# Layernorm statistics and scaling in a four-block tower: from whole-unit VectorE instructions to ScalarE instructions of 128x64

## What is computed

```python
def _layernorm(x, axis=-1, eps=1e-05):
    m = jnp.mean(x, axis=axis, keepdims=True)
    v = jnp.var(x, axis=axis, keepdims=True)
    return (x - m) / jnp.sqrt(v + eps)
...
h = _L0_tok_ref(x, L0_tok_W)
h = h + _L0_attn_ref(_layernorm(h), ...)   # linear attention with a decay mask
h = h + _L0_ffn_ref(_layernorm(h), ...)    # 16 experts, top 2, then a layernorm with gain and bias
h = h + _L1_attn_ref(_layernorm(h), ...)   # 2 heads in blocks of 8 tokens, softmax
h = h + _L1_ffn_ref(_layernorm(h), ...)    # 32 experts, top 1
h = h + _L2_attn_ref(_layernorm(h), ...)   # linear attention, two more layernorms with gain and bias
h = h + _L2_ffn_ref(_layernorm(h), ...)    # 8 experts, top 2, gelu
h = h + _L3_attn_ref(_layernorm(h), ...)   # complex diagonal recurrence
h = h + _L3_ffn_ref(_layernorm(h), ...)    # gated binary weights: signs of sums, "votes"
```

## Time and profile before

| | us |
|---|---|
| median of 3 runs | 701.21 |
| lowest and highest | 699.85, 702.47 |
| the profiled execution, whole | 703.61 |
| its span, first to last instruction | 701.8 |
| mean granted PE clock | 0.886 of full speed |

### The profile page before, as it was taken

How to read it: one execution, slowest core, us unless ns; L and a number is a source line. 1 busy time by engine, 2 the same in 40 slices (tenths; PEclk the granted TensorE clock), 3 DMA queues, 4 the chain that set the end, 5 groups by cost and what they waited for, 6 DMA issues and landing times.

```text
span 701.8 us, 8330 instructions
## 1 busy us (share of the span) xinstructions
PE 582.4 (83%) x2951; PEld 319.9 (46%) x2974; DVE 491.8 (70%) x921; ACT 298.4 (43%) x525; POOL 185.6 (26%) x146
## 2 busy tenths in 40 slices
PE   0378669999999999899589677685897999999996
PEld 0166345444335445366454453345543644444442
DVE  0857779966678998967787988878888973333331
ACT  0222231100011122545356445342455379999985
POOL 6783001000031313420527235425216220000000
PEclk9965569999999999998699887765999999999999
DMA  8310234689564530000000013200420000000011
GB/s 212 105 20 1 60 126 134 211 224 337 189 186 154 160 125 32 1 1 2 0 1 0 1 31 124 75 15 6 162 78 1 1 0 1 1 0 1 0 31 30
DMA packets 30777, 49.85 MB, mean 71 GB/s; under 512 B 8400, under 2 KB 8656, under 8 KB 30736
## 3 DMA queue, kind: packets, MB, share of 16 engines
q1 hardware_dynamic: 29136, 46.82, 21.3%
q10 hardware_dynamic: 576, 1.45, 0.9%
q0 software_dynamic: 1024, 1.05, 0.7%
HBM read 47.86 MB, written 1.44 MB: 70 GB/s over the span
## 4 chain that ended last, share of the span: by engine, by line
PE 54%; DVE 26%; POOL 6%; issue 6%; DMA 4%; ACT 3%; SPq 1%; DVEq 0%; another core or an unknown queue 0%
PE ps L771 9%; PE ps L1032 9%; PE ps L1010 7%; PE ps L764 6%; POOL inv_std L474 4%; PE ps L765 4%; DVE hid L1286 2%; DVE total L1181 2%; PE ps L759 2%; POOL sq L441 2%; DVE xn L1196 2%; PE ps L1021 2%; DVE var L1190 2%; PE ps L886 2%; PE ps L823 2%
## 5 line engine op out<-in xcount | busy, mean ns | idle before, releaser
L711 ACT ACTIVATE hid<-ps 128x512 bf16<-128x512 f32 x256 | 134.0, 619 | 30.4 <-PE ps L1032 29.2
L474 POOL TENSOR_TENSOR inv_std<-var,neg_half 128x8 f32<-128x8 f32 x44 | 79.1, 1798 | 192.1 <-DVE var L1190 191.7
L1032 PE MATMUL ps<-xs,w3z 128*128 128x512 f32 x256 | 118.2, 535 | 5.5 <-DVE xs L1488 3.1
L764 PE MATMUL ps<-xs,up_hi 128*128 128x512 f32 x192 | 97.1, 506 | 21.2 <-DVE hid L1286 13.7
L1010 PE MATMUL ps<-hid,kbin 128*128 128x512 bf16 x248 | 96.2, 391 | 1.0 <-ACT hid L711 0.5
L1488 DVE TENSOR_TENSOR xs<-ps,big_a 128x512 fp32r<-128x512 f32 x64 | 43.5, 689 | 75.3 <-PE ps L1021 72.1
L765 PE MATMUL ps<-xs,up_lo 128*128 128x512 f32 x192 | 79.6, 415 | 0.0
L764 PEld LDWEIGHTS ps<-xs,up_hi 128*128 128x128 f32 x192 | 37.8, 197 | 91.3 <-issue 40.8
L771 PE MATMUL ps<-hid,kb 128*64 128x512 f32 x256 | 69.5, 633 | 0.0
L620 ACT ACTIVATE hid<-ps,kd 128x512 f32<-128x512 f32 x64 | 43.0, 685 | 59.3 <-PE ps L765 34.8
L1032 PEld LDWEIGHTS ps<-xs,w3z 128*128 128x128 f32 x256 | 49.8, 195 | 29.6 <-ACT hid L711 13.1
(11 more groups left out here) (252 smaller groups left out, 973.9 us busy)
## 6 DMA issues: line engine op xcount, KB each, us to landing
big_a<-gates_out SPq DMA_DIRECT2D x64, 256.0 KB, 3.9
fm<-gates_out SPq DMA_DIRECT2D x32, 256.0 KB, 3.9
xT<-gates_out SPq DMA_DIRECT2D x32, 256.0 KB, 3.9
big_a<-gates_out SPq DMA_DIRECT2D x32, 128.0 KB, 2.9
fm<-gates_out SPq DMA_DIRECT2D x16, 128.0 KB, 2.9
xT<-gates_out SPq DMA_DIRECT2D x16, 128.0 KB, 2.9
hid<-wup SPq DMA_DIRECT2D x4, 391.0 KB, 12.5
out<-h SPq DMA_DIRECT2D x4, 256.0 KB, 2.6
```

The lines of the kernel that those rows point to most:

```text
L474: G.tensor_tensor(inv_std[u][:, :], var[u][:, :], neg_half[:, :], ALU.pow).then_inc(norm_rstd[u], 1)
L711: act.activation(sg[u][:, n % SUMS, :], b0, ACT.Sign).then_inc(s_made[u], 1)
L764: pe.matmul(b0, up_hi[:, a:a + P], xs[u][:, l, :], start=True, stop=False)
L1032: pe.matmul(b0, w3z[:, j, 2 * b:2 * (b + 1), :].rearrange("p i o -> p (i o)"), xs[u][:, l, :], start=True, stop=True).then_inc(w_made[u], 1)
```

## The change

The variance and most of the scaling are done elsewhere, and the lists are new:

- `square` now issues eight ACT instructions of 128x64, one for each sequence, in place of one of 128x512 (44 times: four units, eleven layernorms). Each has a bias read from a 128x1 tile, `eps_root`, and an accumulator output: the sum over its 64 elements goes to one column of `var`. The bias is sqrt(1e-5 / 64), so that the squares come with the epsilon.
- DVE's sum of the squares (L1190) is gone, all 44. POOL's `rstd` waits for ACT's last square.
- `square_scale` is `square` and a second step with eight ACT copies of 128x64, in place in `xn`, each with its scale read from a 128x1 column of `inv_std`. It serves A0, M0, A1, M1, A2, IN2, M2, A3 and M3; DVE's L1196, 36 instructions, is gone. IN0 and OUT2 keep DVE's multiplication.
- `sq` loses its 65th column, and POOL's setup fills `eps_root` once where it filled that column in four tiles.
- All five strings of `TURNS` are new.

```diff
--- before.py
+++ after.py
+EPS_ROOT = (LN_EPS / 64.0) ** 0.5
...
     "ACT": (
-        "sss00100211100031222011011ttt323322333232300000100110110011021020110302003020123011301322101002112321311"
+        "sss0000020202002200ttt1123121312233321121133331310300000000000000000202002022020012020133121312130322031"
...
+        eps_root = sb("eps_root", [P, 1])
...
-        sq = per_unit("sq", [P, SEQS, D + 1])
+        sq = per_unit("sq", [P, SEQS, D])
...
-        NORM_SUM, NORM_CEN, NORM_VAR, NORM_OUT, NORM_N = 1, 2, 3, 4, 4
+        NORM_SUM, NORM_CEN, NORM_OUT, NORM_N = 1, 2, 3, 3
...
-                    for n in units:
-                        G.memset(sq[n][:, :, D:D + 1], LN_EPS)
+                    G.memset(eps_root[:, :], EPS_ROOT)
                     G.memset(neg_half[:, :], -0.5).then_inc(eps_set, 1)
...
                     def rstd(ln):
                         yield
-                        pool.wait_ge(norm_step[u], norm_at(ln, NORM_VAR))
+                        pool.wait_ge(norm_sq[u], ln + 1)
                         G.tensor_tensor(inv_std[u][:, :], var[u][:, :], neg_half[:, :], ALU.pow).then_inc(norm_rstd[u], 1)
...
                     def square(ln):
                         yield
+                        if ln == LN_A0:
+                            act.wait_ge(eps_set, 1)
                         act.wait_ge(norm_step[u], norm_at(ln, NORM_CEN))
-                        act.activation(sq[u][:, :, 0:D], xn[u][:, :, :], ACT.Square, scale=float(D) ** -0.5).then_inc(norm_sq[u], 1)
+                        for j in range(SEQS):
+                            last = act.activation(sq[u][:, j, :], xn[u][:, j, :], ACT.Square, scale=float(D) ** -0.5,
+                                                  bias=eps_root[:, :], accum_out=var[u][:, j:j + 1])
+                        last.then_inc(norm_sq[u], 1)
+
+                    def square_scale(ln):
+                        yield from square(ln)
+                        yield
+                        act.wait_ge(norm_rstd[u], ln + 1)
+                        for j in range(SEQS):
+                            last = act.activation(xn[u][:, j, :], xn[u][:, j, :], ACT.Copy, scale=inv_std[u][:, j:j + 1])
+                        last.then_inc(norm_step[u], 1)
...
-                    yield from square(LN_A0)
+                    yield from square_scale(LN_A0)
...
                         V.scalar_tensor_tensor(xn[u][:, :, :], spread(total[u][:, :], D), -1.0 / D, src[u][:, :, :],
                                                ALU.mult, ALU.add).then_inc(norm_step[u], 1)
-                        yield
-                        if u == 0 and ln == LN_A0:
-                            dve.wait_ge(eps_set, 1)
-                        dve.wait_ge(norm_sq[u], ln + 1)
-                        V.tensor_reduce(var[u][:, :], sq[u][:, :, :], X, ALU.add).then_inc(norm_step[u], 1)
 
                     def norm(ln, src, ready, value):
                         yield from centred(ln, src, ready, value)
-                        yield
-                        dve.wait_ge(norm_rstd[u], ln + 1)
-                        V.tensor_tensor(xn[u][:, :, :], xn[u][:, :, :], spread(inv_std[u][:, :], D),
-                                        ALU.mult).then_inc(norm_step[u], 1)
```

More of the change, by code:

```diff
@@ L59 @@
+        "30320320121021031023023123102103102302312310210310230213210320103102321302102301021320320120310320123123"
+        "23131212312323131212312323131212312323131212312323131212312323131212312323131212312323123113133131131331"
+        "3113131333"
     ),
     "PE": (
[L61 to L62 removed]
@@ new lines @@
+        "20302310231313001301301311310331213123312313130213013320330011213132030231022322212221123220213320012311"
+        "13102312302131321302131300130133020302300201101303131320302011012033302020021200221001320020020230030022"
+        "00100210231003100110032001301100330012003130012301300200130032000310030000100210320000100320010320022002"
+        "23002200302200200221002200220120023200122001300221102231100223110023311002233100223310122331100223110023"
+        "31100223130022331012233110022311002331100221330022110332211003322003112003311002213302211330022110022330"
@@ L81 @@
+        "30031333333000020223000000000000000222020222222010110033302220222121010013311313101130323030330000002121"
+        "22201022202222222313321222122133030302212121111111120131131112333323131313131313230333333323221110131323"
+        "21312322021232232111203223331110111133221113023333313131032330121130332103210321032102301230123123123123"
+        "123123123123131313"
     ),
@@ L225, in view @@
             return ap[:, a:a + n].rearrange("p (j e) -> p j e", **sizes)
-        y = [sq[u][:, :, 0:D] for u in units]
+        y = [sq[u][:, :, :] for u in units]
         shifted = [view(fm2[u], 0, W, e=D) for u in units]
@@ L629, in program @@
                     act.activation(v[u][:, :, 0:LANES * D], per_tile(b0), ACT.Copy).then_inc(act_step[u], 1)
-                    yield from square(LN_M0)
+                    yield from square_scale(LN_M0)
                     yield from turned_parts(X_M0)
@@ L639, in program @@
                     yield from square(LN_IN0)
-                    yield from square(LN_A1)
+                    yield from square_scale(LN_A1)
                     yield from turned(X_A1)
@@ L655, in program @@
                     act.activation(wbd[u][32:64, :, 32:64], s32[u][32:64, :, :], ACT.Copy).then_inc(act_step[u], 1)
-                    yield from square(LN_M1)
+                    yield from square_scale(LN_M1)
                     yield from turned_parts(X_M1)
@@ L667, in program @@
                     act.activation(fm[u][:, :], b1, ACT.Relu).then_inc(act_step[u], 1)
-                    yield from square(LN_A2)
+                    yield from square_scale(LN_A2)
                     yield from turned(X_A2)
@@ L678, in program @@
                     act.activation(kf2[u], per_tile(b0), ACT.Relu).then_inc(act_step[u], 1)
-                    yield from square(LN_IN2)
+                    yield from square_scale(LN_IN2)
                     yield
@@ L686, in program @@
                     yield from square(LN_OUT2)
-                    yield from square(LN_M2)
+                    yield from square_scale(LN_M2)
                     yield from turned_parts(X_M2)
@@ L697, in program @@
                     act.activation(fm[u][:, :], b1, ACT.Copy).then_inc(act_step[u], 1)
-                    yield from square(LN_A3)
+                    yield from square_scale(LN_A3)
                     yield from turned_parts(X_A3)
-                    yield from square(LN_M3)
+                    yield from square_scale(LN_M3)
                     yield from turned(X_M3)
```

41 lines of the change are left out of this document (15 added, 26 removed).

## The result

| us | before | after |
|---|---|---|
| median of 4 runs, same chip | 700.53 | 725.73 |
| lowest and highest | 697.67, 702.47 | 722.70, 728.25 |
| the profiled execution's span | 701.8 | 726.0 |

The account below looks back on a forecast made before the run. No single engine was taken to bound the kernel: PE bounds the second stretch, ACT takes DVE's lead in the third. +3 - 9 + 2 - 5 = -9 us gave 694.6 us on the profiled execution, 692 by the median, range 666 to 718.

Parts of the forecast that it names:

- A square: On ACT, one 128x64 square with accumulator output was to hold the engine 0.35 us, eight 2.8 us.
- A product: On ACT, one 128x64 product with its scale read from a tile was to take 0.25 us, eight 2.0 us.
- 2.9 us more: Each layernorm's added latency from ACT's squares and products, said to hide while other units have work on every engine.
- 0 to M0: First stretch, to unit 3's layernorm M0: one layernorm's latency shows at A0, where nothing runs beside it, +3 us.
- M0 to A1: Second stretch, experts of the first block: PE bounds and loses 8.6 us of work to the new lists, -9 us.
- A1 to M3: Third stretch, 272 us before: ACT replaces DVE as fullest engine, so DVE's relief buys nothing; 274 us, +2.
- leaders' sum: Third stretch cut in six parts: busy times of each part's fullest engine added, 234 us forecast against 232.3 before.
- The share of it: Third stretch: the fullest engines' summed busy time over its length, 0.854 before, assumed the same after the change.
- M3 to the end: Last stretch, only votes: 215 instead of 223 stand behind unit 3's M3, at 0.60 us each, -5 us.
- the rival: The slower case: ACT's square groups stand before other units' activations or signs, so PE waits; 714 us, chance 0.27.
- ACT's bursts set the pace: Third stretch: square groups on ACT delay other units' activations and signs, +21 to +33 us; 714 us, chance 0.27.
- ACT stays cover: Third stretch: short instructions fit ACT's gaps and PE sets the time, -20 in place of +2; 670 us, chance 0.22.
- no effect: Third stretch held by unit order and latencies, ACT's longer chain cancelling DVE's relief; 701 us, chance 0.09.

Follow-up runs that it names:

- experiment 6: Kernel before with five memsets of 128x512 on POOL ahead of each power, nothing added on ACT, DVE or PE: 803.19 us, ratio 1.1489.
- the power in parts: Kernel after with POOL's power cut in two or four, each part started when its squares are done: 710.66 us (two), 713.76 us (four).

## Why the prediction was wrong

**The durations were right.** A square 0.35 forecast, 0.33 measured (bounds 2.0 and 3.7 us for eight, measured 2.65). Its accumulator step 0.10, measured 0.09. A product 0.25 and 0.24. ACT's busy time 475 and 461 us, DVE's 434 and 436. The four new table loads take 1.28 us each.

**The step that failed** is "2.9 us more, with POOL's 1.8 us unchanged between the earlier trace rows. While the other units have work on every engine this hides." The 2.9 us were about right (2.7 in the median, 2.1 in the mean), but they don't hide: experiment 6 has 104 of 126 us of such latency in the time with the lists of before, and the power in parts gives back 0.3 to 0.6 us for one with the lists of after. The forecast also left out that ACT now stands in front of its products while POOL works, 20 us in all. The premise was wrong, because cover needs an engine that may take up other work while one unit is late. Here the next instruction of PE's list is fixed, and if it is a transpose that waits for a product, all that stands behind it waits too. The kernel before said so: its rows for L759 had 26 us of PE waiting for products in a chain of 6.7 us, and the forecast didn't ask what this row does when the chain grows.

**0 to M0:** +3 forecast, +10.5 measured. Only A0 of one unit was charged, though this stretch holds seven whole layernorms and the start of the eighth, and PE is busy there for only 68 of the 115 us. With the lists of before the stretch is 120 us, five longer, and with those of after 123.5 even with the old code, so most of this goes with the lists.

**M0 to A1:** -9 forecast, -5.4 measured. Sign and cause right: PE binds there, and it has 9.1 us less to do (171.0 to 161.8); its idle time there rose from 10.0 to 13.8 us.

**A1 to M3:** +2 forecast, +14.6 measured. The leaders' sum was forecast at 234 us and is 238.0 (35.79 + 58.96 + 31.48 + 27.31 + 57.38 + 27.12). The share of it fell from 0.854 to 0.830: the sum's 4 us are worth 5, and the lower share 8. A share carried over from the kernel before assumes that the waits between engines stay as they are, and it was the waits that the change altered. PE leads four of the six parts, where the recorded sum took 33, 54, 33, 28 and 57 us of ACT and 29 of DVE and none of PE, although PE led two of them before; that 234 is near 238 is luck in part. PE's 227.6 us are 11 more than before, at a granted clock of 0.79 and not 0.84 (11 missing rows of before are up to 4 of them). The old code with the new lists has 226.9 us at 0.80 there, so this goes with the lists. Its stretch is 281 us long: of the 14.6 us some 9 come with the lists and 5.5 with the code on them.

**M3 to the end:** -5 forecast, +4.3 measured. ACT takes 219 votes behind M3's centring, where 223 stood before and 215 were forecast, so half of the gain in votes was there. But the stretch starts slowly, on the layernorms of two units in front of and between the votes. The first 12 us behind the cut, before and after:

```profile
568.00:580.00 12.00, 11.69 (x48) 5.42 (x47) 8.01 (x13) 9.99 (x20) 1.64 (x1) 1.00 0.00 0
```

```profile
587.70:600.00 12.30, 7.92 (x33) 3.47 (x33) 3.36 (x5) 11.87 (x43) 2.72 (x2) 1.00 0.00 0
```

PE has 7.9 of 12.3 us and ACT 11.9, while in the kernel before PE has 11.7 of 12.0. Votes wait for bursts there: this is the mechanism of the rival, in a place where ACT is simply full.

**The rivals.** "ACT's bursts set the pace" came nearest with 714 us, 12 below the measured time. Of the lines that were named, the transposes behind L606 did show up (30.5 us); the up matmuls behind L635 hardly did (7.5 us, and 6.9 before). It tied the loss to a price of 0.40 us for a square; the squares cost 0.33 and the loss came all the same. "ACT stays cover" and "no effect" fell. None of the rivals had the latency as its mechanism, except "no effect", which named it and netted it to nothing.

## What to carry to other kernels

Where every engine runs a fixed list, the latency added to a chain is priced from the waits for its last instruction, and not from the room on any engine: find in the list of waits who waits for that chain, and charge a part of the added latency for each time it runs, until an experiment shows cover. Here 0.3 to 0.8 us of each us of it appeared in the time. An engine at 43% busy is no free place if short evictions of other units stand in its list; a burst of 2 to 3 us can delay each of them, and so can a wait of that engine inside the chain. When code and order change together, time the new code with the old order and the other way round before reasoning about either.

## What the runs showed of the hardware that was not expected

- An accumulator output on ACT is a second row, `ACTIVATION_READ_ACCUMULATOR`, of 190 ns. It overlaps its square, and the pitch (from one start to the next) is 0.33 us against 0.24 for a product, or a square, of the same shape without it. What the Trainium skill says of VectorE (VectorE: DVE Perf Modes, Two Vector instructions with no wait between them), that an accumulator output makes two instructions of one, these rows show for ACT.
- POOL's power took 1.64 us for 128x8, 1.01 for 128x4 and 0.69 for 128x2 (medians): 0.37 us plus 0.16 for each column. The versions with it in parts that overlap the squares were 7 to 15 us faster, though four parts take 2.8 us of POOL where one took 1.6.
- Eight ACT products of 128x64, each with a scale read from a tile, take 2.0 us, where one square of 128x512 holds the engine for 0.53 us.
